# A graph network's set-up: loads and weights reordered, one branch instead of two, the code for sorted inputs directly behind it

## What is computed

```
edge_attr = swish(edge_attr_raw @ enc_W + enc_b)
for _ in range(4):
    e_in = concat([edge_attr, x[src], x[dst]])
    edge_attr += layernorm(swish(e_in @ eW1 + eb1) @ eW2 + eb2, eg, ebeta)
    agg = segment_sum(edge_attr, dst)
    x_new = layernorm(swish(concat([x, agg]) @ nW1 + nb1) @ nW2 + nb2, ng, nbeta)
    x = x + x_new
return layernorm(x0 + x)
```

## Time and profile before

| | us |
|---|---|
| median of 3 runs | 2559.54 (2553.31 to 2559.95) |
| profiled execution | 2559.71 |
| its span, first to last instruction | 2557.9 |
| set-up, until the first table product | 0 to 58.4 |
| table loop and first matrices | 58.4 to 95.7 |
| edge groups and node steps | 95.7 to 2557.9 |

### The profile page before, as it was taken

The page is one execution under the profiler, slowest core; times in us unless marked ns, Lnnn a source line. Parts: engine busy times, 40 slices in busy tenths (PEclk is TensorE's granted clock), DMA queues, the critical chain, the costliest instruction groups (busy, mean ns, idle before and its releaser), DMA issues.

```text
span 2557.9 us, 82623 instructions
## 1 busy us (share of the span) xinstructions
PE 2362.3 (92%) x27988; PEld 1851.8 (72%) x27988; DVE 2229.6 (87%) x6144; ACT 1912.1 (75%) x5248; POOL 1625.1 (64%) x1588
## 2 busy tenths in 40 slices
PE   1799999999979999999987999999997999999995
PEld 0477777777747788888865788778874788788874
DVE  5599999999865999999964999999984799999997
ACT  1577777777647888888845888888864888888874
POOL 1377777777307777777604777777721777777750
PEclk9999999999999999999999999999998999999998
DMA  2666666666437888888725888888844666667740
GB/s 87 201 190 205 200 202 200 207 207 204 125 131 215 247 258 255 258 254 252 236 93 182 245 252 253 254 252 254 259 140 144 198 207 203 202 202 205 205 144 26
DMA packets 382979, 515.23 MB, mean 201 GB/s; under 512 B 58489, under 2 KB 256412, under 8 KB 382546
## 3 DMA queue, kind: packets, MB, share of 16 engines
q1 hardware_dynamic: 307282, 304.22, 36.5%
q0 software_dynamic: 75264, 205.62, 29.2%
HBM read 390.55 MB, written 119.05 MB: 199 GB/s over the span
## 4 chain that ended last, share of the span: by engine, by line
PE 37%; POOL 34%; issue 12%; DVE 9%; DMA 5%; ACT 2%; SPq 1%; DVEq 0%; ACTq 0%; POOLq 0%
POOL arena L1612 34%; PE psum L1653 8%; PE psum L1680 7%; PE psum L1641 6%; DMA arena<-node_tables,idx_all 3%; PE psum L1711 3%; PE psum L2103 3%; PE psum L1633 3%; PE psum L1665 2%; DVE arena L1907 2%; PE psum L2142 2%; PE psum L2116 2%; SPq L326 1%; DVE arena L1927 1%; PE psum L1675 1%
## 5 line engine op out<-in xcount | busy, mean ns | idle before, releaser
L1612 POOL DMA_INDIRECT arena<-node_tables,idx_all x1568 | 1616.1, 1031 | 821.5 <-issue 435.8
L1776 ACT ACTIVATE arena<-psum 128x1024 f16<-128x1024 f32 x392 | 401.0, 1023 | 406.6 <-PE psum L1653 406.6
L1866 DVE SCALAR_TENSOR_TENSOR arena<-psum,arena 128x1024 f16<-128x1024 f32 x392 | 478.7, 1221 | 153.0 <-PE psum L1680 88.9
L1680 PE MATMUL psum<-w_hi,arena 128*128 128x128 f16 x6272 | 589.3, 219 | 3.9 <-DVE arena L1866 3.9
L1680 PE MATMUL psum<-w_lo,arena 128*128 128x128 f16 x3136 | 545.5, 219 | 0.0
L1680 PEld LDWEIGHTS psum<-w_hi,arena 128*128 128x128 f16 x6272 | 498.3, 98 | 17.0 <-DVE arena L1866 5.2
L1653 PE MATMUL psum<-arena,w_hi 128*128 128x512 f16 x1568 | 469.9, 382 | 1.5 <-ACT arena L1813 1.5
L1641 PE MATMUL psum<-ident,arena 128*128 128x128 f16 x6272 | 418.1, 220 | 34.0 <-DMA arena<-node_tables,idx_all 33.3
L1641 PEld LDWEIGHTS psum<-ident,arena 128*128 128x128 f16 x6272 | 381.2, 98 | 57.8 <-DMA arena<-node_tables,idx_all 49.4
L1789 ACT ACTIVATE arena<-psum 128x128 f32<-128x128 f32 x1568 | 412.6, 290 | 5.5 <-PE psum L1680 5.5
L1777 ACT ACTIVATE psum<-psum 128x1024 f32<-128x1024 f32 x392 | 399.5, 1019 | 0.0
(11 more groups left out here) (184 smaller groups left out, 3077.5 us busy)
## 6 DMA issues: line engine op xcount, KB each, us to landing
state<-arena SPq DMA_DIRECT2D x294, 256.0 KB
arena<-state SPq DMA_DIRECT2D x294, 256.0 KB
arena<-node_tables SPq DMA_DIRECT2D x784, 64.0 KB
arena<-matrices SPq DMA_DIRECT2D x294, 128.0 KB
node_tables<-arena SPq DMA_DIRECT2D x100, 256.0 KB, 2.2
arena<-node_tables,idx_all POOLq DMA_INDIRECT x1568
arena<-rel_rows SPq DMA_DIRECT2D x98, 128.0 KB
matrices<-arena SPq DMA_DIRECT2D x98, 128.0 KB
```

What stands on the lines that cost most here:

```text
L1612: pool.indirect_dma_start(out=rows[n % R][:, t, :], out_offset=None, in_=p_table, in_offset=bass.IndirectOffsetOnAxis(ap=idx_all[:, n % G1 ...
L1680: x = pe.matmul(ps_v(k2)[:, t * P:(t + 1) * P], h[k2][:, half, t * P:(t + 1) * P], w[:, half, :], start=False, stop=half == 1 and h is hl, ...
L1776: act.activation(hh[k2], ps_h(k2), ACT.Silu).then_inc(S("hh"), 1)
L1866: dve.scalar_tensor_tensor(hl[k2], ps_h(k2), 1.0, hh[k2], ALU.mult, ALU.subtract).then_inc(S("hl"), 1)
```

## The change

One branch per engine is left, in `general_or_not`; it stands directly behind `flag`, asks for the opposite (`< 1`), and the sorted code follows it. `general_*` moves into the other arm, together with the `phase` wait and `enc_bd`, `enc16`. The group columns become `group_*` and are called in both arms.

In the set-up: lists in 96 + 1 + 1 rows and attributes in 112 + 13 rows (`WHOLE`, `PARTS`); x and the three parts of `eW1` are issued by ScalarE; the load of `v_row` and its work are gone; `attr16` is written before the branch; `agg_deg` is cleared by GpSimd, `rel_all` by VectorE behind the branch. `p_bias` and `beta_w1` are made ahead of the column copies. The other weights are cut in four (`weight_parts`) and done inside the table loop behind tiles 4, 8, 13 and 17; the copies of a bias to four places are one instruction with a broadcast input. The `phase` wait of the sorted code is replaced by single waits where the data is used. `tmpw`, `tmpv` and `red` get space of their own.

```diff
+EVEN = 16
+PARTS = ((0, EP // EVEN * EVEN), (EP // EVEN * EVEN, EP))
+WHOLE = (G1 - 1) // EVEN * EVEN
...
         def setup_sp(sp):
-            load(d_int[0:G1 - 1, :], dst_in[0:(G1 - 1) * GE].rearrange("(g e) -> g e", e=GE), "dst")
...
+            for tile, edges, name in ((d_int, dst_in, "dst"), (s_int, src_in, "src")):
+                for a, b in ((0, WHOLE), (WHOLE, G1 - 1)):
+                    load(tile[a:b, :], edges[a * GE:b * GE].rearrange("(g e) -> g e", e=GE), name)
+                load(tile[G1 - 1:G1, 0:LAST], edges[(G1 - 1) * GE:E].rearrange("(g e) -> g e", g=1), name)
...
+            for a, b in PARTS:
+                load(attr_32[a:b, :], flat[a:b, :], "attr")
...
-            sp.wait_ge(SU("flag"), 1)
-            with sp.If(sp.value_load(flag[0:1, 0:1], min_val=0, max_val=1) > 0):
-                general_sp(sp)
-            with sp.Else():
-                sp.nop()
-
+            for part, count, rows in ((0, 1, attr_hi), (2, 1, attr_hi), (1, 2, attr_lo)):
+                sp.wait_ge(SU("split"), count)
+                for a, b in PARTS:
+                    sp.dma_start(attr16[part:part + 1, :].rearrange("a (p c) -> p (a c)", p=EP)[a:b, :], rows[a:b, :]).then_inc(SU("attr"), 16)
+
+        def group_sp(sp):
             sp.wait_ge(SU("rel"), 1)
             sp.dma_start(rel_rows[:, :], rel16[0:G2, :]).then_inc(SU("relrow"), 16)
...
-            sp.wait_ge(SU("attr"), 64)
             sp.wait_ge(SU("relrow"), 16)
-            sp.wait_ge(SU("cols"), 4)
-            sp.wait_ge(SU("weights"), 1)
-            sp.wait_ge(SU("split"), 8)
-            sp.wait_ge(SU("xcopy"), 1)
-            sp.sem_inc(phase, 1)
...
+            sp.wait_ge(SU("attr"), 16 * 4 * len(PARTS))
...
         def setup_pool(pool):
...
+            pool.memset(agg_deg[:, :, :], 0.0).then_inc(SU("pads"), 1)
...
         def setup_dve(dve):
...
-            done(dve.memset(agg_deg[:, :, :], 0.0))
...
-            done(dve.memset(rel_all[:, :, :], 0.0))
...
+        def group_dve(dve):
...
+            done2(dve.memset(rel_all[:, :, :], 0.0))
             done2(dve.tensor_copy(d_grp, d_int))
...
+            dve.wait_ge(SU("w"), NW)
+            pair_p_bias(done2, dve)
+            dve.wait_ge(SU("betaw"), 1)
+            done2(dve.tensor_copy(beta_w1[:, :], psum[0:1, 1, 0:H]))
+            dve.sem_inc(SU("p_bias"), 1)
+            dve.wait_ge(SU("groupT"), 1)
             dve.tensor_copy(rel_all[:, :, 0:G2], psum[:, 2, :].rearrange("p (t g) -> p t g", t=TPG)[:, :, 0:G2]).then_inc(SU("cols"), 1)
...
         def setup_act(act):
-
-            act.wait_ge(SU("attr"), 16)
+            whole = N // P
+            for t in range(0, whole, 4):
+                act.dma_start(x0_all[:, t:t + 4, :], x_in[t * P:(t + 4) * P, :].rearrange("(t p) f -> p t f", p=P)).then_inc(SU("x"), 16)
+            act.wait_ge(SU("xzero"), 1)
+            act.dma_start(x0_all[0:N - whole * P, whole, :], x_in[whole * P:N, :]).then_inc(SU("x"), 16)
+            act.dma_start(w_pq[:, 0, :], eW1[D:2 * D, :]).then_inc(SU("w"), 16)
...
+            act.wait_ge(SU("attr"), 16 * len(PARTS))
             act.copy(attr_hi, attr_32).then_inc(SU("split"), 1)
...
             def begin_pe(self, pe):
...
+                pe.wait_ge(SU("xcopy"), 1)
                 turn(0)
                 turn(1)
+                pe.wait_ge(SU("const"), 4)
+                pe.wait_ge(SU("p_bias"), 1)
+                pe.wait_ge(SU("cols"), 4)
...
             def begin_act(self, act):
...
+                act.wait_ge(SU("split"), 2)
+                act.wait_ge(SU("attr"), 16 * 4 * len(PARTS))
                 turned(0)
...
             def begin_dve(self, dve):
...
+                first_layer, second_layer, node_layer, biases = weight_parts(dve)
                 for t in range(NT):
...
+                    if t == 4:
+                        first_layer()
+                    if t == 8:
+                        second_layer()
+                    if t == 13:
+                        node_layer()
+                    if t == 17:
+                        biases()
...
-        def general_or_not(eng, then, otherwise=lambda: None):
-            with eng.If(eng.value_load(flag[0:1, 0:1], min_val=0, max_val=1) > 0):
-                then()
+        def general_or_not(eng, then, otherwise):
+            eng.wait_ge(SU("flag"), 1)
+            with eng.If(eng.value_load(flag[0:1, 0:1], min_val=0, max_val=1) < 1):
+                otherwise()
             with eng.Else():
                 eng.nop()
-                otherwise()
+                then()
```

More of the change, by code:

```diff
@@ L182, in build_program @@
         ntf = take(CH)
+        tmpw = take(GE)
+        tmpv = take(GE)
+        red = take(16)
         cut[0] = 0
@@ L353, in setup_sp @@
+            load(nbeta_row[:, :], nbeta.partition_broadcast(P), "w")
+            for k in range(2):
+                load(nb1_col[:, k:k + 1], nb1[k * P:(k + 1) * P].rearrange("(p a) -> p a", a=1), "w")
             load(tmpv[0:1, 2 * D:3 * D], eb2.rearrange("(a f) -> a f", a=1), "w")
             load(tmpv[0:1, 3 * D:4 * D], nb2.rearrange("(a f) -> a f", a=1), "w")
[L355 to L358, removed]
@@ L404, in general_sp @@
             sp.wait_ge(GS("attr_out"), 16)
+            group_sp(sp)
+            sp.wait_ge(SU("cols"), 4)
+            sp.wait_ge(SU("x"), NX)
+            sp.wait_ge(SU("w"), NW)
+            sp.wait_ge(GS("weights"), 1)
+            sp.wait_ge(SU("split"), 8)
+            sp.wait_ge(SU("xcopy"), 1)
+            sp.sem_inc(phase, 1)
         def setup_pool(pool):
@@ L477, in setup_dve @@
             done(dve.memset(red, 0.0))
+            done(dve.memset(wide_col[:, :], 0.0))
+            dve.memset(x0_all[:, N // P, :], 0.0).then_inc(SU("xzero"), 1)
             done(dve.memset(p_bias[:, :], 0.0))
@@ L512, in setup_dve @@
             dve.tensor_scalar(flag[0:1, 0:1], red[0:1, 4:5], float(HALF_N - 1), None, ALU.is_gt).then_inc(SU("flag"), 1)
-            dve.wait_ge(SU("flag"), 1)
[L514 to L517, removed]
+        def group_dve(dve):
             c2 = SU("dve2")
@@ L567, in centre @@
                 done(dve.tensor_scalar(cols, cols, -1.0 / D, None, ALU.mult))
-            enc = enc_bd[:, :, :].rearrange("a t f -> a (t f)")
-            rows17 = TPG * RAW + 1
-            done(dve.memset(enc16[:, :], 0.0))
-            for row in (0, 64):
-                done(dve.tensor_copy(enc16[row:row + rows17, :], enc))
-            done(dve.tensor_tensor(enc16[32:32 + rows17, :], enc, enc16[0:rows17, :], ALU.subtract))
-            centre(w2, red[:, 5:7])
-            for k in range(2):
-                done(dve.tensor_scalar(w2[:, k, :], w2[:, k, :], red[:, 5 + k:6 + k], None, ALU.add))
@@ L595, in setup_dve, with first_layer, second_layer @@
-            dve.wait_ge(SU("betaw"), 1)
-            done(dve.tensor_copy(beta_w1[:, :], psum[0:1, 1, 0:H]))
-            pair_p_bias(done, dve)
-            dve.sem_inc(SU("weights"), 1)
+            def first_layer():
+                done(dve.tensor_copy(w1_hi[:, :], tmpw[:, 0:H]))
+                done(dve.tensor_tensor(w1_lo[:, :], tmpw[:, 0:H], w1_hi[:, :], ALU.subtract))
+            def second_layer():
+                w2 = tmpv[:, 0:2 * D].rearrange("p (k f) -> p k f", k=2)
+                centre(w2, red[:, 5:7])
+                for k in range(2):
+                    done(dve.tensor_scalar(w2[:, k, :], w2[:, k, :], red[:, 5 + k:6 + k], None, ALU.add))
+                done(dve.tensor_copy(w2_hi[:, :, :], w2))
+                done(dve.tensor_tensor(w2_lo[:, :, :], w2, w2_hi[:, :, :], ALU.subtract))
@@ L1726, in pe @@
                     pe.wait_ge(Z("tab_lo"), NT)
+                    pe.wait_ge(SU("weights"), W_OPS)
                 turn(first)
@@ L2337, in step @@
                 end_phase()
+            presort(eng)
+            eng.wait_ge(phase, 1)
             first_init(eng)
@@ L2365, in _ @@
             setup_sp(sp)
-            sp.wait_ge(phase, 1)
-            general_or_not(sp, lambda: general_steps(sp, I1.sp, I2.sp, nothing, S1.sp, S2.sp, node_mid.sp, node_end.sp, end_phase, False), fast)
+            general_or_not(sp, lambda: general_steps(sp, general_sp, I1.sp, I2.sp, nothing, S1.sp, S2.sp, node_mid.sp, node_end.sp, end_phase, False), fast)
         @block.gpsimd
```

171 lines of the change are left out of this document (83 added, 88 removed).

## The result

The change makes the kernel faster: 2535.3 us (median of 9 runs, 2523.33 to 2541.97) against 2557.54 us (9 runs, 2546.72 to 2559.95) beside it. The ratio is 0.9908, 95% interval 0.9889 to 0.9928, so 23.5 us less, give or take 5 (the medians lie 22.2 apart). Forecast were 27.6 us less and 2532.

What follows compares the result with a forecast made beforehand. TensorE was taken to bind the edge stretches, busy 2142.50 of 2229.00 us, with the change reaching only the first 96 us and the end. A to E sum to 33.3; 33.3 - 2 - 3.7 = 27.6 us less gives 2532, range 2523 to 2545.

Steps and rivals of the forecast that it cites:

- A: Set-up, target list: spread over engines it lands at 6.5 us, so the sorted-input test starts earlier; saves 5.7 us.
- B: Set-up, branch behind the flag: sorted code follows without a jump, 1.2 us instead of 5.48; saves 3.8 us.
- C: Set-up, group columns: `p_bias` and `beta_w1` now come ahead of the column copies; costs 3.1 us.
- D: Set-up, weights from 32.17 to 49.07 us: waiting and work leave VectorE's path; saves 16.9 us.
- E: Set-up, attribute-write wait and second branch, 49.07 to 59.12 us: they leave VectorE's path; saves 10.05 us.
- F: Table loop: 7.8 us of weight work in four parts placed there, mostly hidden in gaps; costs 2 us.
- the first three fit into the gaps: Table loop: weight parts of 0.65, 1.95 and 1.3 us fit gaps of some 2 us; 1.9 of the last sticks out.
- G: Kernel's end: sorted code jumps over the other code, SP's own jump uncovered; costs 3.7 us.
- Late inputs: Rival, set-up: list lands behind x (costs 3.5 us), weights or attribute write bind (2.5 more); 2538 us, chance 0.20.
- The turned branch does nothing: Rival, branch: code behind it is fetched as late as far code, price at the end stays; 2536 us, chance 0.12.
- Slower: Rival, edge stretches: TensorE is granted less clock in the body, 1.5% lost; 2565 us, chance 0.05.
- the signs named: Trace marks: gather near 64 us, L1533 near 26, test near 6.7, ScalarE waits about 4, edge stretches within 5.

Runs made afterwards that it cites:

- e3: Changed kernel with `agg_deg` cleared by VectorE in two halves while it waits, instead of by GpSimd; 2529.71 us, executed once.
- e5: Changed kernel with the edits of e3 and e4 together; median 2529.43 us, ratio 0.9885 to the kernel before.
- e1: Changed kernel with the branch turned back, so unsorted code stands behind it and sorted code far off; ratio 0.9916 to the kernel before.
- e2: Kernel before with only its last branch turned round, so sorted code stands directly behind it; ratio 0.9991 to the kernel before.
- e7: Changed kernel with the lists in 97 rows and a last one again, as before; 2549.01 us, executed once.
- e6: As e5, with GpSimd's subtraction `attr_lo` held back until VectorE has the shifted targets, for sorted inputs only; 2522.75 us, executed once.
- e4: Changed kernel without weight work in the table loop: two operations in front of the first matrices, 22 behind the loop; 2529.17 us, executed once.
- e10: As e5, but w1 behind tile 4, the tail of e9, and `attr_lo` made after `p_bias`; median 2523.77 us, ratio 0.9863 to the kernel before.
- e12: e10 with its branch turned back, so the sorted code lies far off; ratio 0.9881 to the kernel before.
- e9: Changed kernel with SP's three waits for the last output writes behind both arms of the branch; 2530.28 us, executed once.
- e8: Changed kernel with x issued by SP behind its other loads, as before; eW1 parts stay with ScalarE; 2535.43 us, executed once.
- e11: Changed kernel run once more, unedited, beside e10; median 2538.41 us, ratio 0.9903 to the kernel before.

## Why the prediction was right, and where its steps were off

The sign, the range and the place were right: the gain came from the first 96 us. By the two first traces the sum was 3.7 us too high, and the terms say where. That the profiled execution took 2531.88, just the 2532 of the forecast, is luck: 4.0 us of its gain lie in the body, where none was forecast.

*A, the target list, 4.1 instead of 5.7.* With x beside it the list had landed by 6.6 us in e3, at 6.9 in e5 and at 7.4 in the changed kernel, where 6.5 was taken: close, but some 0.7 us of the missing 1.6 are the list. The other 0.9 failed in the sentence that clearing `agg_deg` on GpSimd costs nothing, or 0.3 us if each of VectorE's operations beside it is slowed by a tenth. The cast wasn't slowed by a share, it was held for the whole of the memset and ended with it. e3 took the memset away and had the cast back at 0.23 us.

*B, the branch, 3.8 and 3.8.* 1.16 us against 1.2. e1 (5.54) and e2 (0.17 instead of 4.05) show that the price hangs on the order of the code. The 5.48 us of the earlier trace rows stood behind a jump over some 200 instructions, where a wait for the source list comes next, and the prediction left open which of the two they were. The trace of the kernel before tells. VectorE's sequencer did nothing between its branch at 19.7 us and this (ns, start us):

```profile
L528 DVEq EVENT_SEMAPHORE  x1: 21/21/21, 24.1 to 24.1; - x1
```

The last step of the source list's semaphore is at 21.5 us in that trace, 2.6 us earlier. In e7, where the code stood right behind the branch, VectorE went on 0.16 us after that step (26.58, memset at 26.75), and its row names the list, as the row of the kernel before doesn't. So the empty 4.4 us were the jump's; the list lay under it, and would by itself have ended the wait some 2.5 us sooner (an estimate from these two rows). For the forecast 3.8 both had to go, and both went. The Trainium skill's window of 512 instructions (Runtime: NRT & Kernel Launch, section "Instruction fetch mechanics"), as the prediction read it, would have made this jump free; the trace doesn't agree.

*C, the group columns, -4.8 instead of -3.1.* From the shifted targets (22.28) to the last copy (29.03) passed 6.75 us; 6.7 were worked out. Of the missing 1.7 us, 1.5 are L521 beside GpSimd's subtraction. e6 moved the subtraction and with it the stall. In the kernel before, the subtraction ran from 29.77 to 32.98, beside VectorE's copies out of PSUM, and nothing stalled; the change brought the attributes forward until it fell among operations on SBUF. This is the same missed rule as in A.

*D and E, 26.9 and 26.95.* Right, mechanism and size: no wait stands there any more.

*F, the table loop, -3.4 instead of -2.* The loop has 3 us more, 0.2 fewer lie in front of it, and 0.6 more behind its last write. Before, the write landed 0.3 us ahead of the gather at 95.68:

```profile
93.21 2.18 DMA node_tables<-arena
```

Now the gather starts 0.9 us behind it (the 0.88 us of "issue" above); why isn't known. The step "the first three fit into the gaps" was wrong. The waits for ScalarE (9.8 us before, 5.7 now) fell by 4.1 us while 6.3 us of work went in, and e4 has the loop 3.5 us shorter without it. This is clear of the scatter: from the memset that starts the sorted code to the gather, the seven traces with all these weights in the loop take 39.2 to 42.4 us, those of e4, e5, e6, e10 and e12, of e2 and of the kernel before 36.6 to 38.1. The probable reason is that a late tile makes its write late, for which ScalarE waits four tiles on: the writes run at 205 GB/s with the weights and at 227 without. The work itself was sized too high, 7.8 us from a stretch's length (14.30) where VectorE's busy time in it was 12.65.

*G, the end, -2.8 instead of -3.7.* The mechanism was right, the size somewhat high (2.4 to 2.8 in e1, e2 and e9), and e9 shows both where it sits and that moving the last waits hides it.

*The rivals.* "Late inputs" didn't come in its size: x beside the list held it up by at most some 2 us (it landed at 5.3 us in e8, and at 6.1 to 7.6 in the changed kernel, e1, e4, e9 and e11), not 3.5, and VectorE waited for no weight and no attribute write. "The turned branch does nothing" was wrong in its mechanism (the code behind was there) and close in its effect: with its price at the end the turn is worth 1.4 us by the traces. "Slower", by the clock, didn't come: the mean granted clock over the nine runs is 0.982 to 0.986, and from the first gather to the last issue the kernel takes as long as before, within what e11 differs from the first trace.

*Of the signs named*, the first gather was expected near 64 and came at 69.0, L1556 at 29.1 instead of 26, the test at 8.29 instead of 6.7, and the waits for ScalarE at 5.7 us instead of 4; 1.16 us behind the flag and SP's last branch 3.0 us ahead of the end came as said. The body differed by 4 us. The bound of 5 us set for it was too narrow: the same kernel passes it between two executions (9 us, e11).

What the runs leave open: the body of the seven executions with the weights in the loop averages 2457.6 us, that of the five with them behind it 2452.8. With a scatter of 4 us that is a hint that e10's surplus (14.6 us against the changed kernel by the medians, 8.1 by gather and tail against the first trace, 10.7 against e11's) has a part in the edge groups; it isn't shown.

## What to carry to other kernels

Before an idle GpSimd is given a long operation, look at what VectorE does in these microseconds: in these traces casts, `tensor_scalar` on two columns or more and, beside the subtraction, an operation with two inputs in SBUF stopped for the whole of it; copies out of PSUM and reductions went on. When a set-up is reordered, the sum of its parts is not enough; each transfer that lands earlier starts its reader earlier, beside other work. And when a branch is turned so that the used code follows it, its end becomes a jump: put the last waits behind both arms, so that the jump lies under them.

## What the runs showed of the hardware

- GpSimd held VectorE off for whole instructions. Beside GpSimd's memset of 5.42 us, which only writes, a cast of 0.23 us took 5.22. Beside its subtraction of 3.22 us, operations of 0.17, 0.43 and 0.16 us took 1.64 to 3.32; a `tensor_reduce` of 0.69 us and a `tensor_scalar` on one column (0.15 us) inside it kept their times, as did copies out of PSUM (0.67 and 1.01 us in e10). The Trainium skill (SBUF — State Buffer, section "Who interferes with whom") states this rule: an exclusive lock on a shared port pair, held for the instruction, by `cast` and `tensor_scalar` in their two-port modes, and by two SBUF inputs against a GpSimd instruction that reads. The rows here agree; that a `tensor_scalar` on one column isn't held, that section doesn't say. The prediction missed the rule.
- The start of far code behind a taken branch cost VectorE 3.9 us (e2), 4.4 (e1) and 5.0 (e12 against e10), a jump over some 200 instructions 4.4 too (the kernel before), and the jump at the end 2.4 to 2.8 on SP (e1, e2, e9). Where the engine waits for a transfer meanwhile, the price hides (e9).
- A list of 97 rows moved at 26 GB/s, one of 96 rows and one apart landed at 6.1 to 7.6 us beside x, at 5.3 without (e8); taken back, the two lists held VectorE 11.0 us longer (e7).
- The same program differed by 9 us between the first gather and the last issue, and by 2.5 us in its table work, from one execution to another (e11).
